# Variance matmuls in groups of four slots instead of two, on a graph network with layer norms

## The reference

```python
hi = jnp.einsum('bsh,hk->bsk', x, W1[:H])
hj = jnp.einsum('bsh,hk->bsk', x, W1[H:])
h = jax.nn.relu(hi[:, :, None, :] + hj[:, None, :, :] + b1)
y = jnp.einsum('bijk,kl->bijl', h, W2) + b2
y = _layernorm(y, gamma, beta)
out = jnp.einsum('bij,bijh->bih', adj, y)
```

## Time and profile before

| | |
|---|---|
| runs (3) | 3257.77, 3257.95, 3258.49 us; median 3257.95 us |
| profiled execution, span | 3262.8 us |
| granted TensorE clock, mean | 0.991 |
| busy: TensorE, VectorE, ScalarE, GpSimd | 3114.7, 2913.6, 2498.6, 2330.6 us |
| L400 products, 4096 instructions | 2111.0 us, mean 597 ns |
| L411 variance matmuls, 4096 | 545.5 us, mean 605 ns |
| L548 squares, 2048 | 1357.9 us, mean 682 ns |

### The profile page before, as it was taken

How to read it: one execution, slowest core, us unless ns; L and a number is a source line. 1 busy time by engine, 2 the same in 40 slices (tenths; PEclk the granted TensorE clock), 3 DMA queues, 4 the chain that set the end, 5 groups by cost and what they waited for, 6 DMA issues and landing times. The chain is left out here.

```text
span 3262.8 us, 75153 instructions
## 1 busy us (share of the span) xinstructions
PE 3114.7 (95%) x12162; PEld 1224.6 (38%) x12162; DVE 2913.6 (89%) x20494; ACT 2498.6 (77%) x4612; POOL 2330.6 (71%) x3529
## 2 busy tenths in 40 slices
PE   8999999999999999999999999999999999999995
PEld 3333333333333333333333333333333333333332
DVE  5998898898988988989989889889898898898997
ACT  7777777777777777777777777777777777777773
POOL 7777677777776776777767767777677677777772
PEclk9999999999999999999999999999999999999996
DMA  1000000000000000000000000000000000000000
GB/s 27 9 13 10 10 11 10 12 10 10 12 10 10 12 9 12 11 10 12 10 10 12 9 11 11 10 12 10 10 12 10 10 11 10 12 10 10 12 10 7
DMA packets 152776, 35.86 MB, mean 11 GB/s; under 512 B 116737, under 2 KB 152449, under 8 KB 152449
## 3 DMA queue, kind: packets, MB, share of 16 engines
q1 hardware_dynamic: 152448, 33.11, 4.9%
HBM read 18.29 MB, written 4.19 MB: 7 GB/s over the span
## 5 line engine op out<-in xcount | busy, mean ns | idle before, releaser
L400 PE MATMUL y_ps<-h,w2c 128*128 128x512 f32 x4096 | 2111.0, 597 | 19.6 <-ACT h L539 19.6
L663 DVE CUSTOM_DVE_ANT_0 h<-h,cb_ps 128x128 f32<-128x128 f32 x8192 | 1878.8, 277 | 30.8 <-PE cb_ps L422 28.1
L842 POOL TENSOR_TENSOR pre<-vT,uT 128x384 f32<-128x384 f32 (+1 forms) x2048 | 1854.0, 937 | 21.6 <-ACT vT L532 10.9
L548 ACT ACTIVATE sq<-y_ps,b2c_col 128x512 f32<-128x512 f32 x2048 | 1357.9, 682 | 34.8 <-PE y_ps L400 32.4
L539 ACT ACTIVATE h<-pre 128x896 f32<-128x896 f32 x1024 | 969.2, 946 | 353.4 <-DVE h L650 336.3
L400 PEld LDWEIGHTS y_ps<-h,w2c 128*128 128x128 f32 x4096 | 722.3, 192 | 257.5 <-issue 201.4
L422 PE MATMUL cb_ps<-c_rows,pick 96*128 96x512 bf16 x2048 | 789.1, 386 | 22.3 <-DVE gT L663 16.0
L663 DVE DVE_READ_ACCUMULATOR2_ANT gT<- 128x1 f32 x8192 | 651.8, 80 | 47.9 <-issue 47.9
L650 DVE TENSOR_SCALAR h<-vT,uT 128x128 f32<-128x128 f32 x1024 | 496.6, 486 | 122.7 <-issue 121.9
L411 PE MATMUL ss_ps<-sq,sel 128*32 128x512 f32 x4096 | 545.5, 605 | 0.1
L422 PEld LDWEIGHTS cb_ps<-c_rows,pick 96*128 96x128 bf16 x2048 | 197.6, 96 | 858.3 <-DVE gT L663 521.7
(11 more groups left out here) (95 smaller groups left out, 1930.6 us busy)
## 6 DMA issues: line engine op xcount, KB each, us to landing
devs<-dev_rows SPq DMA_DIRECT2D x512, 8.0 KB
c_rows<-c_part SPq DMA_DIRECT2D x384, 16.0 KB, 1.8
x_in<-in_x_dram SPq DMA_DIRECT2D x64, 64.0 KB, 1.8
adj_c<-in_adj_dram SPq DMA_DIRECT2D x64, 64.0 KB, 1.9
c_pair<-c_row_sum SPq DMA_DIRECT2D x256, 0.2 KB, 1.7
adj_in<-in_adj_dram SPq DMA_DIRECT2D x64, 64.0 KB, 1.8
x_res<-in_x_dram SPq DMA_DIRECT2D x64, 64.0 KB, 1.9
out_dram<-x SPq DMA_DIRECT2D x64, 64.0 KB, 1.6
```

The costliest lines, as they stand in the source:

```text
L400: pe.matmul(y_ps[:, t % 2, c0:c0 + COLS], w2c[:], h[:, t, c0:c0 + COLS], start=True, stop=True).then_inc(y_done, 1)
L548: act.activation(sq[:, t % SQ_RING, c0:c0 + COLS], y_ps[:, t % 2, c0:c0 + COLS], ACT.Square, bias=b2c_col[:], scale=float(P) ** -0.5).then ...
L663: op = dve.tensor_tensor_reduce(h[:, t, cols], h[:, t, cols], cb_ps[:, block_of_duo, k * P:(k + 1) * P], 1.0, 0.0, ALU.mult, ALU.add, gT[: ...
L842: op = pool.tensor_tensor(pre[:, t % PRE_RING, c0:c0 + units * P].rearrange("p (i j) -> p i j", j=P), vT[:].rearrange("p (o j) -> p o j", ...
```

## The change

Three things: squares of a slot are made by one activation of 1024 columns over two PSUM banks, at the start of ScalarE's slot s for slot s-2 (the call for block 0 of slot s-1 goes); the ring `sq` has eight slots; and `variances` covers four slots with sixteen matmul instructions, called in slots 1, 5, 9 and 13 for slots s-5 to s-2. The semaphore counts follow. `deviations` stays in slots 2 and 10.

```diff
-SQ_RING = 4
+SQ_RING = 8
+GROUP = 4
...
-                    wait(pe, sq_done, 2 * (SLOTS * g + t - 1))
+                    wait(pe, sq_done, SLOTS * g + t - 1)
...
-                half, p = t // HALF, (t % HALF) // 2
-                wait(pe, sq_done, 2 * (SLOTS * g + t + 2))
-                if p == 0:
+                half = t // HALF
+                wait(pe, sq_done, SLOTS * g + t + GROUP)
+                if t % HALF == 0:
                     wait(pe, dev_done, 2 * g + half)
-                for q in range(4):
-                    c0 = (q % 2) * COLS
-                    mm = pe.matmul(ss_ps[32 * q:32 * q + 32, :], sel[:, ROWS - 1 - p:ROWS - 1 - p + 32],
-                                   sq[:, (t + q // 2) % SQ_RING, c0:c0 + COLS],
-                                   start=(p == 0), stop=(p == ROWS - 1))
+                for pair in range(GROUP // 2):
+                    p = (t % HALF) // 2 + pair
+                    for q in range(4):
+                        c0 = (q % 2) * COLS
+                        mm = pe.matmul(ss_ps[32 * q:32 * q + 32, :], sel[:, ROWS - 1 - p:ROWS - 1 - p + 32],
+                                       sq[:, (t + 2 * pair + q // 2) % SQ_RING, c0:c0 + COLS],
+                                       start=(p == 0), stop=(p == ROWS - 1))
                 mm.then_inc(var_summed, 1)
...
-                    sg, t = (new, s - 3) if s >= 3 else (old, s + SLOTS - 3)
-                    if s % 2 == 1 and sg is not None:
+                    sg, t = (new, s - 5) if s >= 5 else (old, s + SLOTS - 5)
+                    if s % GROUP == 1 and sg is not None:
                         variances(sg, t)
...
-            def squares(g, t, block_of_duo):
-
-                wait(act, y_done, 2 * (SLOTS * g + t) + block_of_duo + 1)
-                if block_of_duo == 0:
-
-                    wait(act, var_summed, SLOTS // 2 * g + (t - SQ_RING) // 2 + 1)
-                c0 = block_of_duo * COLS
-                act.activation(sq[:, t % SQ_RING, c0:c0 + COLS], y_ps[:, t % 2, c0:c0 + COLS], ACT.Square,
+            def squares(g, t):
+
+                wait(act, y_done, 2 * (SLOTS * g + t) + 2)
+                wait(act, var_summed, SLOTS // GROUP * g + (t - SQ_RING) // GROUP + 1)
+                act.activation(sq[:, t % SQ_RING, :], y_ps[:, t % 2, :], ACT.Square,
                                bias=b2c_col[:], scale=float(P) ** -0.5).then_inc(sq_done, 1)
...
-                wait(act, var_summed, SLOTS // 2 * g + HALF // 2 * (half + 1))
+                wait(act, var_summed, SLOTS // GROUP * g + HALF // GROUP * (half + 1))
...
-                        squares(sg, t, 1)
+                        squares(sg, t)
...
-                    sg, t = (new, s - 1) if s >= 1 else (old, SLOTS - 1)
-                    if sg is not None:
-                        squares(sg, t, 0)
```

## The result

The changed kernel takes 3453.48 us (median of 4, 3449.74 to 3456.64) against 3258.22 us of the kernel before beside it (3257.77 to 3259.23): ratio 1.0598, 95% interval 1.0583 to 1.0613. It is slower, as forecast, but by 195 us, not 117 us, and outside the range (to 3440 us).

What follows compares the result with a forecast made beforehand. TensorE and VectorE were taken to lead by turns. Groups +2.25 and squares +0.15 us over 63 graph steps (151 us), loop turn -0.58 us over 59 trips (-34 us): +117 us, 3375 us, range 3295 to 3440 us.

Steps and rivals of the forecast that it cites:

- The double group: Sixteen matmuls in slots 1, 5, 9, 13: the second half was to cost 0.86 us, at most 1.09 us.
- the 0.23 us of a drain: Extra cost in slots 1, 9 and 13 if the array drains between a double group's halves; +43 us in all.
- Slot 1, +0.86: Longer group delays slot 2's broadcasts; VectorE, without slack there, starts slot 3 late: +0.86 us per graph.
- Slot 9, +0.86: Longer group delays the deviations and their DMA, so invs starts later: +0.86 us on top of slot 1's delay.
- Slots 11 and 13, +0.53: Slot 11's group goes, regaining 0.33 us before VectorE's late block stops TensorE; slot 13's double group adds 0.86 us.
- Slots 3, 5, 7: 0: Groups gone in slots 3 and 7, double in slot 5: no change, as VectorE has work in hand.
- Squares and the turn of the loop, +0.15 - 0.58: Whole squares delay slot 7's aggT, +0.15 us per graph; L650 ends after GpSimd's third addition, not fourth, -0.58 us per trip.
- Slot 15: 0: Removing the group before L448 gains nothing: TensorE already waits there; its 1.10 us idle becomes about 2.2 us.
- Rivals 1 and 2: 1: TensorE bounds throughout, 3199 us, chance 0.08; 2: late groups and gains both absorbed, within 0.2% of 3258 us, 0.05.
- rival 5: Double group drains between halves (3418 us), or a whole square takes 1.38 us (3392 us); chance 0.08.
- Rival 3: Unseen slack in the deviation chain or slot 2: 3321 us without one +0.86 us term, 3267 without both; chance 0.17.
- rival 4: At the loop's turn L650 misses GpSimd's third addition: +1.0 us over 59 trips, 3434 us; chance 0.14.

## Why the prediction was right and wrong

The forecast of slower held, and so did its mechanism: the groups' total work falls, but TensorE's microseconds are worth something only where it leads, and the change takes them out of slots where VectorE leads or TensorE idles and adds them in slots 1, 9 and 13. Slot by slot in the profile, point by point:

- *The double group.* The sixteen matmuls take 1.93 us, and from the product to the next broadcast it is 2.81 us (1587.33 to 1590.14) against 1.95 us: the second half costs 0.86 us. Right: the 0.23 us of a drain does not show inside it. This agrees with what the prediction takes from the Trainium skill, "TensorE: Matmul & The Clock Gate", Step-by-step: what each phase is for, on weight loads.
- *Slot 1, +0.86.* Measured +0.95 (one split) and 0.7 to 0.8 in the kernel before (one moved). Right.
- *Slot 9, +0.86.* Measured 0.6. The chain through the DMA is real but carries less than half, 0.2 to 0.3 us; I had put invs's new wait at 1 us, it is near 0.4. Another 0.2 us is the ReLU's wait, which I had not seen; what agreement there is between 0.6 and 0.86 is in part luck.
- *Slots 11 and 13, +0.53.* Measured 0.57. Right.
- *Slots 3, 5, 7: 0.* No run tests them singly. In the two traces slots 2 to 8 together take 21.4 us against 21.3 us, and the terms sum up without them: 61 + 40 + 36 + 4 (squares) + 54 (clock) = 195 us. That this meets the measured 195 us to the last one is luck: the terms come from different sessions and are good to some 5 us each.
- *Squares and the turn of the loop, +0.15 - 0.58.* Put at -25 us, measured +4 us. **This failed, by 29 us:** L650 does end earlier, but a second gap of "issue" lies three sums later, and I had left its row out of the argument. The end of that gap did not move. The 4 us are the squares' price in the kernel before; beside the double groups it is 26 us, and the difference is inside the terms of the splits.
- *Slot 15: 0.* **The step that failed most, by 54 us.** I wrote that the idle time of 1.10 us becomes about 2.2 us, and priced that at nothing. It does become so, and it takes the clock away in 33 of 59 trips. The Trainium skill, "TensorE: Matmul & The Clock Gate", HAM oscillation (HAM is its name for the clock gate), describes a kernel whose waits between bursts of matmuls bring the clock down again in every turn of its loop; here the trace shows it in 33 of 59 trips, and in the kernel before in none. Corrected, the sum is 117 + 54 + 29 - 14 (slot 9) + 7 (slot 1) + 3 (slots 11 and 13) = 196 us, the same terms as above and so no second check of them.

Rivals 1 and 2 were excluded by the sign, and rival 5 by the group of 1.93 us and the square of 1.11 us. Rival 3 holds in a small part, for slot 9. The price of rival 4, 3434 us, came nearest, for another reason: L650 took under 0.6 us in 43 of the 59 trips, so it mostly did not miss the third addition. Of what I said the profile would show, the group of under 2 us, L548 at 1.11 us, TensorE's idle time of 2 us and the waits of broadcasts in slots 4, 8 and 12 came (0.1, 0.1 and 0.4 us per graph); the wait of 1 us at invs did not.

What stays open: which trips lose the clock, and why a split in slot 9 or 13, which leaves the idle time ahead of slot 1 as it is, lowers their number from 33 to 15 and 14. Idle times of 1.63 to 2.63 us ahead of L451 stand in trips with and without the loss, in the same kernel, and all idle time of TensorE in slot 0 together is 2.2 to 2.6 us in both kinds. So the length of the idle time does not settle it; nothing here was run to settle it.

## What to carry to other kernels

Where two engines share the lead, price an edit by the slot: ask who leads there, and what a bunch of work pushes behind it; fewer and larger groups save little per boundary (0.23 us here) and push a whole group (0.86 us) onto whoever waits. Idle time of TensorE is not free when it grows: check the granted clock behind every stretch that a change makes longer. And look for the place where an engine idles anyway; joined there, a double group gained 0.5%.

## What the runs showed of the hardware

- A clock loss that comes and goes: with 1.10 us idle ahead of L448 in no trip, with 2.2 us and more in 14 to 33 of 59 trips, 1.64 us each, so that a microsecond more of idle time, off the path by itself, cost 54 us. Filling it with useless products of 128 columns (1.3 us per graph) brings all of that back, though some 1.0 us of idle time is left.
- A jump of VectorE's loop costs two gaps in the next graph, 2.07 us ahead of the first instruction and 0.8 to 1.3 us some instructions later (121.9 and 47.9 us in 59 trips before), while no matmul of TensorE, which has a loop of its own, waits for "issue". Half the jumps away is 44 us, 1.35%.
- An activation of 1024 columns over two PSUM banks takes 1112 ns against 2 x 682 ns, what the slope of the ReLUs gave (1.11 us).
